# Edge lookups in adj: a bit table read by TensorE in place of 80 indirect DMAs, with host-made transposes

## The chip, the cores and the metric

One core of one Trainium2 chip runs the kernel. The metric is the device time of one execution in microseconds (us). It has five engines with their own instruction streams: PE (TensorE, matmul), DVE (VectorE), ACT (ScalarE), POOL (GpSimd) and SP (SyncE, here only a DMA queue). They wait for each other by semaphores. DMA transfers are issued from SP, ACT and POOL.

## The reference

`x` is 1354 x 512, `adj` a 0/1 matrix of 1354 x 1354 with about four other ones in a row and ones on the diagonal. The list of 10,000 edges (pairs of rows) is random; only an edge that is also in `adj` changes a softmax score, and there are fewer than 64 of those.

```python
q = (x[sub] @ Wq.T + bq).reshape(-1, 8, 64)
k = (x[obj] @ Wk.T + bk).reshape(-1, 8, 64)
att = ((q * k).sum(-1) / 8).T
scores = zeros((8, n, n)).at[:, sub, obj].set(att)
scores = where(adj == 0, -inf, scores); scores[:, i, i] = 1e-07
x1 = layernorm(x + (softmax(scores, 2).sum(0) / 8) @ x)
out = layernorm(x1 + adj @ (x1 @ W1) + b1)
```

## The kernel before, in words

Rows of `x` and `adj` stand in T = 11 tiles of 128 rows (the last has 74). Numbers that need more than fp16 are split in a high and a low half, so most products are two matmuls.

**First stage, sums.** Without edges every softmax row is uniform, so the first layer is a sum over neighbours. SP loads `adj` tile by tile into `stage` (a ring of 3), ACT casts it (L628), PE transposes it in 11 pieces (L1113), ACT copies that into `adjT` (L619). PE makes the sums of tile i with 22 matmuls of 512 columns (L1134); the first two tiles' sums are interleaved and wait for the tiles of `x` as DVE splits them (L809). DVE adds the row's own share (L884), takes its moments (L829, L830), ACT the root (L633) and the normalised row (L663), DVE splits it (`x1s`, L895 and L897).

**Second stage, mix.** 12 units of 11 steps, each step two matmuls (L1191), make `adj @ x1`: 8 units of 512 columns, then 4 of 330. `mix_rows(a, b)` in PE's program are steps a to b - 1 of these 132. ACT and DVE take each unit out of PSUM (L716, L864), four banks in turn.

**Third stage, output.** For each tile 12 matmuls with `W1` (L1273) and 2 with the rank-64 correction (L1280), then DVE adds (L1078), takes moments, ACT roots and scales (L764), and SP stores.

**Edges.** In parallel POOL looks up all 10,000 edges in `adj`: 80 indirect DMAs of 125 elements (L560), in six chunks. DVE waits for a chunk and makes flags (`flag_chunk`, L840), PE numbers the flagged edges (L481, L482) and compacts them (L489), between the work above. Each engine takes its instructions in order, so a wait for flags on DVE also holds the normalisation behind it. After the last chunk come the steps on the 64 found edges: gather rows of `x`, project (L1230), dots (L1242), softmax (L1246, exp), shares (L1250), corrected rows (`dx1`, L1056), the correction's product (L1261). They stand between steps of the mix at places written by hand. Where there are more than 64 such edges a general path runs (`overflow`); it is not taken here, but its branch is.

Of the kernel before, what the change touches and what calls it, by code (L numbers as in the profile page):

```python
# [4 lines left out]

N = 1354
# [12 lines left out]
CHUNKS = [0, 16, 32, 48, 64, 73, EC]  # L32
NC = len(CHUNKS) - 1
CHUNK = max(b - a for a, b in zip(CHUNKS, CHUNKS[1:]))

NUMBERED_AT = {4: 0, 6: 1, 8: 2, T: 3, T + 1: 4, T + 2: 5}
FLAGGED_AT = {3: 0, 5: 1, 8: 2, T - 1: 3}
# [6 lines left out]
CASTS = 2  # L44
SUMS = 4
COEFS = 4
# [10 lines left out]
def resnorm_graph(nc, x, adj, pairs, wq, bq, wk, bk, w1, b1, out):  # L57
    f32, f16, i32 = mybir.dt.float32, mybir.dt.float16, mybir.dt.int32
    ALU, ACT, AX = mybir.AluOpType, mybir.ActivationFunctionType, mybir.AxisListType
    width = [P] * (T - 1) + [LAST]  # L60

    with ExitStack() as ctx:
# [5 lines left out]

        sums_dram = nc.dram_tensor("sums_dram", [NP, GW], f32, kind="Internal").ap()
# [10 lines left out]
        stage = sb("stage", [P, RING, N])  # L80
        room16 = sb("room16", [P, CASTS * NP], f16)
        adj16 = room16[:, 0:CASTS * N].rearrange("p (c n) -> p c n", c=CASTS)
        sums = sb("sums", [P, SUMS, H])
        counts = sb("counts", [P, T, 2])
        wraw = sb("wraw", [P, 3, KF, H])
# [6 lines left out]

        co = sb("co", [P, COEFS, 8])

        st = sb("st", [P, 2, 12])
        last_st = sb("last_st", [P, 12])
        onehot = sb("onehot", [P, P * CHUNK], f16)
        stackL = sb("stackL", [P, NP], f16)
        junk16 = stackL[:, 0:P]
# [8 lines left out]
        slot_no = sb("slot_no", [P, P, CHUNK], f16)  # L108
# [8 lines left out]
        ok2 = y[:, 0, 0:2 * EC].rearrange("p (c two) -> p c two", two=2)  # L117
        ed_ok = sb("ed_ok", [P, EC])
# [3 lines left out]
        ed_adj = sb("ed_adj", [P, EC])  # L122
        ed3 = sb("ed3", [P, EC, 3], f16)
        flag = sb("flag", [P, EC], f16)
        seen = sb("seen", [P, EC])
        pos = sb("pos", [P, 3, CHUNK])
        pos16 = sb("pos16", [P, CHUNK], f16)
        pos_all = seen[0:EP]
# [7 lines left out]
        raw = wraw[:, :, :, :].rearrange("p a b c -> p (a b c)")  # L136
        at = 2 * KF * H

        def take(n):
            nonlocal at  # L140
            at += n
            return raw[:, at - n:at]
        xsub, xobj, spread, same, keq, vsame, small = map(take, (H, H, H, P, SLOTS, P, 80))
        head_of = take(2)
        assert at <= 3 * KF * H
        at = 0
        EXTRA = SLOTS + 3
# [4 lines left out]
        assert at <= 2 * KF * H  # L152
# [41 lines left out]
        idx_ready, flags_ready, numbered, onehot_ready, compacted = map(sem, ("idx_ready", "flags_ready", "numbered", "onehot_ready", "compacted"))  # L194
        wqk_transposed, wqkT_ready, count_ready = map(sem, ("wqk_transposed", "wqkT_ready", "count_ready"))
# [7 lines left out]
        biased, out_done, z_ready, z_moments, z_root = map(sem, ("biased", "out_done", "z_ready", "z_moments", "z_root"))  # L203
# [14 lines left out]

# [10 lines left out]
        ROW_STEPS = 7 + HEADS * 11 + 3 + 3  # L229
# [31 lines left out]
        def general_pe(pe):  # L261
            mm = nc.tensor.matmul
            with pe.Fori(0, T) as t:
# [47 lines left out]
            pe.wait_ge(turn, FINISHED)  # L311

# [33 lines left out]
        def general_dve(dve):  # L346
# [38 lines left out]

# [113 lines left out]
        def _(sp):  # L499
# [29 lines left out]
            with overflow(sp):  # L529
                general_sp(sp)  # L530
# [782 lines left out]
```

## Time and profile before

| what | value |
|---|---|
| median of 3 runs | 238.35 us (237.59 to 239.12) |
| span of the profiled execution | 238.4 us, 3058 instructions |
| PE busy | 186.1 us (78%) |
| DVE busy | 131.5 us (55%) |
| ACT busy | 87.4 us (37%) |
| POOL busy | 130.4 us (55%) |
| DMA | 24.59 MB, mean 103 GB/s |
| granted TensorE clock in 40 slices | `9999999998556999965785979999979999999995` |

The span is that of one execution taken by the profiler; it agrees with the median. The last line is the clock that PE was granted in each fortieth of the span, in tenths of full speed (5 is the lower of its two levels, 1.2 GHz, 9 the full 2.4 GHz). Two matmuls overlap in part, so a group's busy time is a little under its count times its mean.

### The profile page before, as it was taken

To read this page: it belongs to the slowest core of one execution; us is meant where nothing else is said; L and a number is where in the kernel's file an instruction comes from. 1 tells how busy PE (TensorE), PEld (TensorE's weight loads), DVE (VectorE), ACT (ScalarE), POOL (GpSimd) and SP (SyncE) were. 2 spreads that over 40 slices of the span, in tenths; PEclk is the share of its full clock that TensorE was granted. 3 is DMA by queue.
4 is the path that set the end of the run, shared out by engine and by line. 5 is a ranking of instruction groups with operands and counts; after the bars stand their busy time and mean duration, and the time that the engine had idled before them with its cause. 6 is when DMAs were issued, how large, how long until landed. Compare 5 with 4: busy or idle time off the path is not lost.

```text
span 238.4 us, 3058 instructions
## 1 busy us (share of the span) xinstructions
PE 186.1 (78%) x1075; PEld 100.0 (42%) x1075; DVE 131.5 (55%) x374; ACT 87.4 (37%) x153; POOL 130.4 (55%) x114
## 2 busy tenths in 40 slices
PE   4776999991089989504959799979799969999950
PEld 4533455550064554301433346934336544444440
DVE  4695877850385658004617085079897213666670
ACT  3656998960192864000511101401412211333340
POOL 3878878877778777877778654999000000000000
PEclk9999999998556999965785979999979999999995
DMA  6999996766230157820300004000000000222220
GB/s 194 399 300 320 297 331 179 190 170 104 36 90 2 46 182 243 274 62 1 47 1 4 1 21 142 3 1 0 1 0 3 0 4 5 88 91 88 89 88 25
DMA packets 14924, 24.59 MB, mean 103 GB/s; under 512 B 6012, under 2 KB 6137, under 8 KB 14903
## 3 DMA queue, kind: packets, MB, share of 16 engines
q1 hardware_dynamic: 9046, 20.34, 26.1%
q0 software_dynamic: 2848, 1.10, 5.1%
q10 hardware_dynamic: 3008, 2.90, 3.6%
q8 instruction: 10, 0.16, 0.3%
q14 instruction: 12, 0.09, 0.1%
HBM read 14.61 MB, written 9.63 MB: 102 GB/s over the span
## 4 chain that ended last, share of the span: by engine, by line
POOL 43%; PE 31%; issue 12%; DVE 8%; DMA 2%; ACT 1%; DVEq 0%; POOLq 0%
POOL ed_adj L560 43%; PE acc L1191 12%; PE acc L1273 9%; PE tr L1230 3%; PE tr L1273 2%; PE acc L1280 1%; DMA ed_adj<-in_adj,ed_idx 1%; DMA ed_i<-in_L_gnn_rel_pair_index 1%; PE tr L1261 1%; DVE wraw L989 1%; DVE st L829 1%; DVE wraw L988 1%; DVE slot L1008 1%; DVE wraw L996 0%; PE tr L1246 0%
## 5 line engine op out<-in xcount | busy, mean ns | idle before, releaser
L560 POOL DMA_INDIRECT ed_adj<-in_adj,ed_idx x80 | 104.0, 1301 | 27.4 <-issue 23.8
L1191 PE MATMUL acc<-adjT,x1s 128*128 128x512 f16 (+3 forms) x264 | 61.3, 393 | 0.0
L1134 PE MATMUL acc<-xs,adjT 128*128 128x512 f16 (+1 forms) x176 | 42.7, 399 | 2.1 <-ACT adjT L619 1.3
L1191 PEld LDWEIGHTS acc<-adjT,x1s 128*128 128x128 f16 (+1 forms) x264 | 27.0, 106 | 29.5 <-issue 11.8
L633 ACT ACTIVATE st<-st,eps 128x1 f32<-128x1 f32 x24 | 7.1, 297 | 63.1 <-DVE st L830 62.0
L1134 PEld LDWEIGHTS acc<-xs,adjT 128*128 128x128 f16 (+1 forms) x176 | 17.4, 102 | 23.7 <-issue 3.9
L1273 PE MATMUL acc<-whl,xs 128*128 128x512 f16 (+1 forms) x108 | 23.5, 368 | 2.1 <-issue 2.1
L840 DVE SCALAR_TENSOR_TENSOR flag<-ed_adj,ed_ok 125x16 f16<-125x16 f32 (+2 forms) x6 | 1.0, 173 | 41.8 <-DMA ed_adj<-in_adj,ed_idx 41.8
L1113 PE MATMUL tr<-ident,room 128*128 128x128 f16 (+1 forms) x121 | 9.2, 229 | 15.5 <-ACT room L628 14.9
L1273 PEld LDWEIGHTS acc<-whl,xs 128*128 128x128 f16 x108 | 10.5, 98 | 13.9 <-issue 2.5
L628 ACT ACTIVATE room<-stage 128x1354 f16<-128x1354 f32 x11 | 14.7, 1333 | 4.5 <-DMA stage<-in_adj 4.5
L1113 PEld LDWEIGHTS tr<-ident,room 128*128 128x128 f16 (+1 forms) x121 | 7.9, 104 | 19.4 <-ACT room L628 17.6
L619 ACT COPY adjT<-tr 128x1024 f16<-128x1024 f16 (+1 forms) x22 | 15.4, 754 | 1.8 <-PE tr L1113 1.8
L1134 PE MATMUL tr<-xs,adjT 128*128 128x512 f16 (+1 forms) x66 | 14.7, 379 | 0.0
L481 PE MATMUL acc<-flag,below 125*128 125x16 f16 (+2 forms) x6 | 1.1, 182 | 17.3 <-DVE flag L840 17.3
L608 POOL TENSOR_TENSOR x_sb<-x_sb,bias 128x512 f32 x11 | 14.4, 1346 | 0.3 <-POOL stackL L602 0.3
L716 ACT ACTIVATE xs<-acc 128x512 f16<-128x512 f32 (+1 forms) x12 | 6.3, 540 | 20.6 <-PE acc L1191 20.5
L829 DVE BATCH_NORM_STATS2 st<-y 128x6 f32<-128x512 f32 x17 | 11.8, 695 | 0.6
L864 DVE SCALAR_TENSOR_TENSOR xs<-acc,xs 128x512 f16<-128x512 f32 (+1 forms) x12 | 7.3, 620 | 5.9 <-ACT xs L716 5.9
L663 ACT ACTIVATE x_sb<-y,st 128x512 f32<-128x512 f32 x11 | 9.0, 821 | 1.1 <-DVE st L835 1.0
L1134 PEld LDWEIGHTS tr<-xs,adjT 128*128 128x128 f16 (+1 forms) x66 | 6.3, 98 | 7.1
L834 DVE RECIPROCAL st<-st 128x1 f32<-128x1 f32 x24 | 3.9, 161 | 9.1 <-ACT st L633 9.1
(195 smaller groups left out, 248.3 us busy)
## 6 DMA issues: line engine op xcount, KB each, us to landing
stage<-in_adj SPq DMA_DIRECT2D x10, 677.0 KB, 7.4
adjT_dram<-adjT SPq DMA_DIRECT2D x11, 352.0 KB, 3.0
sums_dram<-sums ACTq DMA_DIRECT2D x11, 256.0 KB, 3.6
x_sb<-in_x SPq DMA_DIRECT2D x3, 768.0 KB, 9.0
out<-y SPq DMA_DIRECT2D x6, 256.0 KB, 2.0
ed_adj<-in_adj,ed_idx POOLq DMA_INDIRECT x80, 3.4
wraw<-in_L_gnn_Wq SPq DMA_DIRECT2D x1, 1024.0 KB, 17.8
wraw<-in_L_gnn_Wk SPq DMA_DIRECT2D x1, 1024.0 KB, 10.4
```

What stands on the lines that cost most here:

```text
L560: nc.gpsimd.indirect_dma_start(out=ed_adj[0:EP, c:c + 1], out_offset=None, in_=adj_flat, in_offset=bass.IndirectOffsetOnAxis(ap=ed_idx[0:E ...
L608: nc.gpsimd.tensor_tensor(tile, tile, bias[:, :], ALU.add).then_inc(biased, 1)
L619: nc.scalar.copy(adjT[:, 8 * b:8 * b + n, t * P:(t + 1) * P], tr16[b][:, 0:n * P].rearrange("p (k i) -> p k i", k=n)).then_inc(adjT_ready, 1)
L628: nc.scalar.activation(adj16[:, t % CASTS, :], stage[:, t % RING, :], ACT.Copy, accum_out=counts[:, t, 0:1]).then_inc(adj_cast, 1)
L663: nc.scalar.activation(x_sb[:, i, :], y[:, i % 2, :], ACT.Identity, bias=st[:, i % 2, 9:10], scale=st[:, i % 2, 8:9]).then_inc(x1_ready, 1)
L829: step(V.bn_stats(s[:, 0:6], v))
L864: V.scalar_tensor_tensor(mix[:, 1, u % KF, i:j], mix_bank(u)[:, 0:j - i], 1.0 / XS, mix[:, 0, u % KF, i:j], ALU.mult, ALU.subtract).then_i ...
L1113: last = nc.tensor.transpose(tr16[b][0:width[k], (k % 8) * P:(k % 8 + 1) * P], adj16[:, t % CASTS, k * P:k * P + width[k]], ident16[:])
L1134: last = mm(sum_bank(i)[:, :], adjT[0:width[k], k, i * P:(i + 1) * P], xs[0:width[k], half, k, :], start=(k == 0 and half == 0), stop=(k = ...
L1191: ins = mm(mix_bank(u)[:, 0:j - i], x1s[0:width[k], half, k, f * P:(f + 1) * P], adjT[0:width[k], k, i:j], start=(k == 0 and half == 0), s ...
L1230: last = mm(bank[:, o * SLOTS:(o + 1) * SLOTS], wT[:, n, k, o * P:(o + 1) * P], rows_T[:, k * SLOTS:(k + 1) * SLOTS], start=(k == 0), stop ...
L1273: mm(bank, mix[:, a, k, t * P:(t + 1) * P], whl[:, b, k, columns], start=(k == 0 and n == 0), stop=False)
```

## The change

The 80 lookups go. In their place:

- The host hands over `adj` transposed in tiles (`adj_T`, padded to 1408), its diagonal, and `Wq`, `Wk` transposed. ACT casts each tile straight into `adjT` (1408 columns), and no PE transposes or ACT copies remain for `adj`, `Wq` and `Wk`.
- PE multiplies each `adj` tile with an identity scaled by powers of two (`words`, 11 matmuls of 129 columns): every element of the 128 x 128 result holds 11 bits of `adj`, one for each column tile. DVE folds the 11 results with OR (`fold`) into one table of 128 x 128 words.
- The edges' row numbers mod 128 are written to DRAM and read back onto all partitions (`hot`, 20,000 B on each), the column numbers too (`cols`, 10,000 B on each). DVE turns `hot` into one-hot columns (`hot_part`, 4 pieces). PE multiplies them with the table (`look`, 21 matmuls of 480 columns), DVE masks each by the column (`pick`, 21), PE sums each column (80 matmuls of one column each, with 125 columns of weights taken at a stride of 80 elements).
- The words hold bits of other rows too, so DVE keeps the 8 highest candidates of each partition and POOL looks up these in 8 indirect DMAs.
- The first norm is taken of x + r*S and not of the scaled row, so ACT no longer copies the sums or scales `x` (L645, L671); it now makes the high half of `x1s` as well.
- `Wq`, `Wk` and `W1` are loaded last. POOL adds the bias to `x_sb` before the lookups. In the output six products with `W1` (`base`) now stand ahead of the overflow branch, and the corrections (`finish`) behind it.

```diff
-            for c in range(EC):
-                nc.gpsimd.indirect_dma_start(out=ed_adj[0:EP, c:c + 1], ..., in_=adj_flat, ...)
+            pool.wait_ge(bias_loaded, 16 * BIASES)
+            pool.wait_ge(x1_lo, T)
+            ... (11 adds of bias)
+            pool.wait_ge(top_ready, 1)
+            for c in range(TOP):
+                nc.gpsimd.indirect_dma_start(out=found[0:EP, c:c + 1], ..., in_=adj_flat, ...)
@@ SP
+            load_adj(2)
+            sp.dma_start(aii_all, adj_diag).then_inc(diag_loaded, 16)
+            sp.wait_ge(edges_split, 1)
+            sp.dma_start(row_dram..., row16[0:EP]).then_inc(row_stored, 16)
+            sp.dma_start(col_dram..., col8[0:EP]).then_inc(col_stored, 16)
+            load_adj(3)
+            load_adj(4)
+            load_adj(5)
+            sp.wait_ge(row_stored, 16)
+            sp.dma_start(hot, row_dram.partition_broadcast(P)).then_inc(row_spread, 16)
+            load_adj(6)
+            load_adj(7)
+            sp.wait_ge(col_stored, 16)
+            sp.dma_start(cols[:, :], col_dram.partition_broadcast(P)).then_inc(col_spread, 16)
@@ ACT
+            cast_adj(0); high_x(0); cast_adj(1); high_x(1); high_x(2)
+            cast_adj(2); high_x(3); cast_adj(3)
+            for i in range(T):
+                act.wait_ge(moments_ready, i + 1)
+                act.wait_ge(coefs_ready, i + 1)
+                root(st[:, i % 2], eps_row[:, i:i + 1]).then_inc(root_ready, 1)
+                act.dma_start(sums_dram[...], y4(i)).then_inc(y_stored[i % YS], 16)
+                if i + 4 < T:
+                    cast_adj(i + 4)
+                ... (normalise, high half of x1s)
@@ DVE
+            for t in range(3):
+                split_x(t)
+            dve.wait_ge(diag_loaded, 16)
+            ... (4 small instructions on the diagonal)
+            fold(0)
+            coefs(0)
+            for t in range(3, 6):
+                split_x(t)
+            fold(1)
+            coefs(1)
+            for t in range(6, T):
+                split_x(t)
+            fold(2)
+            for i in range(T):
+                add_sums(i)
+                if i + LEAD + 1 < T:
+                    fold(i + LEAD + 1)
+                if i + 2 < T:
+                    coefs(i + 2)
+                scale_shift_of(i)
+                if i >= 1:
+                    low_x1(i - 1)
+                if 3 <= i < 3 + HOT_PARTS:
+                    hot_part(i - 3)
+                for n in LOOKS_AFTER.get(i, ()):
+                    pick(n)
+            low_x1(T - 1)
+            for n in range(picks, 15):
+                pick(n)
+            mix_low(0)
+            mix_low(1)
+            for n in range(15, LOOKS):
+                pick(n)
@@ PE
+            def look(n):
+                ...
+                if n >= 2:
+                    pe.wait_ge(picked, n - 1)
+                mm(tr[n % 2][...], table[:], hot[:, part], start=True, stop=True).then_inc(looked, 1)
+            keep_warm(40)
+            words(0); sum_neighbours(0, range(0, 3)); words(1); ...
+            words(3)
+            for i in range(2, T):
+                if i + LEAD < T:
+                    words(i + LEAD)
+                sum_neighbours(i, range(T))
+                for n in LOOKS_AFTER.get(i, ()):
+                    look(n)
+            for first, last in MIX_BEFORE_LOOKS:      # ((0, 9), (11, 20), (9, 11), (20, 33))
+                for n in range(first, last, 2):
+                    mix_rows(n, min(n + 2, last))
+                    if looks < LOOKS:
+                        look(looks)
+            mix_rows(MIX_BEFORE_LOOKS[-1][1], 36)
+            pe.wait_ge(picked, LOOKS)
+            for c in range(EC):
+                last = mm(acc[3][0:EP, WORD + c:WORD + c + 1], picked_edge[:, :, c], ones16[:, 0:1], ...)
+            mix_rows(36, 66)
+            pe.wait_ge(flags_ready, 1)
```

What DVE runs at the start of the program, before the change (`x_sb` are rows of x, `xs` their halves, `co` the coefficients of a tile; L798 is the last instruction on edges):

```order
L798 TENSOR_TENSOR ed<-ed,ed_in 125x80x2
L805 TENSOR_SCALAR xs<-x_sb 128x1536
L809 SCALAR_TENSOR_TENSOR xs<-x_sb,xs 128x512 x3
L805 TENSOR_SCALAR xs<-x_sb 128x1536
L809 SCALAR_TENSOR_TENSOR xs<-x_sb,xs 128x512 x3
L818 SCALAR_TENSOR_TENSOR stackL,counts<-room,ident 128x128
```

The same place of the changed kernel (L742 is the last on edges, L809 to L812 those on the diagonal, L754 and L755 a fold, L767 to L770 the coefficients):

```order
L742 SCALAR_TENSOR_TENSOR ed_key<-ed_key,ed_ok 125x80
L804 TENSOR_TENSOR bit_eye<-ident,co 128x11x128
L747 SCALAR_TENSOR_TENSOR xs<-x_sb,xs 128x512 x3
L809 COPY counts<-co 128x11
L810 TENSOR_SCALAR co<-co 128x11
L811 TENSOR_SCALAR co<-co 128x11
L812 SCALAR_TENSOR_TENSOR co<-co 128x11
L754 COPY counts<-tr 128x1
L755 SCALAR_TENSOR_TENSOR folded<-ident,co,tr 128x128
L767 SCALAR_TENSOR_TENSOR co<-counts,co 128x1
L770 SCALAR_TENSOR_TENSOR co<-co 128x1
L747 SCALAR_TENSOR_TENSOR xs<-x_sb,xs 128x512 x3
```

The second and third group of splits now stand behind the instructions on the diagonal, and those behind its load.

What PE runs around the start of the mix, before the change (`room` is the cast adj, `wraw` the weights, `ed` and `onehot` the edges):

```order
L1134 MATMUL acc<-xs,adjT 128x512 x22
L1166 MATMUL acc<-ident,wraw 128x128 x4
L1191 MATMUL acc<-adjT,x1s 128x512 x4
L489 MATMUL acc<-ed,onehot 128x3 x16
L481 MATMUL acc<-flag,below 128x16
L482 MATMUL acc<-flag,ones 128x16
L1191 MATMUL acc<-adjT,x1s 128x512 x34
```

And in the changed kernel (L1099 are sums, L1113 a look, with `hot` in the place of `wraw`, L1153 the mix):

```order
L1099 MATMUL acc<-xs,adjT 128x512 x22
L1113 MATMUL tr<-wraw,table 128x480 x2
L1153 MATMUL acc<-adjT,x1s 128x512 x4
L1113 MATMUL tr<-wraw,table 128x480
L1153 MATMUL acc<-adjT,x1s 128x512 x4
L1113 MATMUL tr<-wraw,table 128x480
```

The numbering and compaction in six rounds has left this place, and a look stands behind every second step of the mix until the 21st.

## Rows read from the trace of the kernel before

**Rows 1.** The page's chain that ended last, by engine.

```profile
POOL 43%; PE 31%; issue 12%; DVE 8%; DMA 2%; ACT 1%; DVEq 0%; POOLq 0%
```

**Rows 2.** The page's groups: busy us, mean ns | idle before, releaser.

```profile
L840 DVE SCALAR_TENSOR_TENSOR flag<-ed_adj,ed_ok 125x16 f16<-125x16 f32 (+2 forms) x6 | 1.0, 173 | 41.8 <-DMA ed_adj<-in_adj,ed_idx 41.8
...
L608 POOL TENSOR_TENSOR x_sb<-x_sb,bias 128x512 f32 x11 | 14.4, 1346 | 0.3 <-POOL stackL L602 0.3
```

**Rows 3.** PE's timeline in the sums: start, us, instructions, [idle before].

```profile
26.11 4.91 PE L1134 MATMUL tr<-xs,adjT 128*128 128x512 f16 x22
30.87 0.78 PE L1113 MATMUL tr<-ident,room 128*128 128x128 f16 x11
...
66.40 1.36 PE L1113 MATMUL tr<-ident,room 128*128 128x128 f16 x11 [11.78 <-ACT room L628]
```

**Rows 4.** Windows: PE, PEld, DVE, ACT, POOL busy, PEclk, DMA share, GB/s.

```profile
58.00:60.00 2.00, 0.00 (x0) 0.00 (x0) 0.00 (x0) 0.00 (x0) 1.65 (x2) 0.57 0.25 50
```

**Rows 5.** The same, of ten microseconds in which DMA was full.

```profile
10.00:20.00 10.00, 8.68 (x47) 3.79 (x45) 6.93 (x17) 5.01 (x9) 8.17 (x7) 1.00 1.05 318
```

**Rows 6.** The tile stage: its loads from SP and their time to landing.

```profile
L514 SPq DMA_DIRECT2D stage<-in_adj x9: 258/328/2781, 4.9 to 47.8; - x9
...
DMA to landing us min/median/max: 4.1/7.4/16.2
```

**Rows 7.** DVE's timeline in the first stage.

```profile
9.06 1.90 DVE L809 SCALAR_TENSOR_TENSOR xs<-x_sb,xs 128x512 f16<-128x512 f32 x3
...
26.85 0.75 DVE L884 SCALAR_TENSOR_TENSOR y<-acc,co,xd 128x512 f32<-128x512 f32 x1
...
28.36 0.18 DVE L830 BATCH_NORM_AGGREGATE st<-st 128x2 f32<-128x6 f32 x1
```

**Rows 8.** PE's timeline around chunks of edges.

```profile
110.76 10.23 PE L1191 MATMUL acc<-adjT,x1s 128*128 128x512 f16 x34
120.83 1.10 PE L489 MATMUL acc<-ed,onehot 125*128 125x3 f16 x16
...
136.43 0.18 PE L481 MATMUL acc<-flag,below 125*128 125x7 f16 x1 [1.68 <-DVE flag L840]
136.49 3.31 PE L1191 MATMUL acc<-adjT,x1s 128*128 128x512 f16 x8
```

**Rows 9.** The chain in order of time: the last lookups.

```profile
131.89 1.22 POOL ed_adj L560
133.41 2.76 DMA ed_adj<-in_adj,ed_idx
```

**Rows 10.** Weight loads of the compaction: ns min/median/max.

```profile
L489 PEld LDWEIGHTS acc<-ed,onehot x80: 140/162/179, 68.2 to 139.9; 125*128 125x128 f16 x80
```

**Rows 11.** PE's timeline behind the last chunk.

```profile
147.32 7.26 PE L1230 MATMUL tr<-wraw,wT 128*128 128x64 f32 x64
...
161.71 9.68 PE L1191 MATMUL acc<-adjT,x1s 128*128 128x512 f16 x44
173.29 1.12 PE L1250 MATMUL tr<-wraw 64*128 64x512 f32 x2 [1.89 <-DVE wraw L1037]
...
187.52 6.91 PE L1191 MATMUL acc<-adjT,x1s 128*128 128x330 f16 x48
196.54 2.77 PE L1273 MATMUL acc<-whl,xs 128*128 128x512 f16 x12 [2.12 <-issue]
```

**Rows 12.** DVE's timeline in the softmax of the found edges.

```profile
162.91 0.69 DVE L998 TENSOR_TENSOR wraw<-tr,wraw 128x512 f32<-128x512 f32 x1
...
165.78 1.22 DVE L1008 TENSOR_TENSOR slot<-wraw 128x1 f32<-128x1 f32 x1
...
172.96 0.28 DVE L1037 TENSOR_SCALAR wraw<-wraw 64x128 f32<-64x128 f32 x1
```

**Rows 13.** DVE's timeline in the output: its last two tiles.

```profile
226.97 0.69 DVE L1078 SCALAR_TENSOR_TENSOR y<-acc,x_sb 128x512 f32<-128x512 f32 x1 [0.61 <-PE acc L1280]
...
229.34 0.42 DVE L1091 SCALAR_TENSOR_TENSOR xd<-acc,x_sb 128x256 f32<-128x256 f32 x1
```

More of the change, by code:

```diff
@@ L43 @@
 RING = 3
[L44 to L46 removed]
+YS = 4
+LEAD = 2
 GW = H + 2
@@ L121, in resnorm_graph @@
         ed_idx = sb("ed_idx", [P, EC], i32)
[L122 to L128, printed above, removed]
+        ed_key = sb("ed_key", [P, EC])
+        ed_bit = sb("ed_bit", [P, EC], i32)
+        ed_word = sb("ed_word", [P, EC], i32)
+        ed_cand = sb("ed_cand", [P, EC])
+        row16 = sb("row16", [P, EC], f16)
+        col8 = sb("col8", [P, EC], u8)
+        hot = wraw[:, :].bitcast(f16)[:, 0:E]
+        cols = sb("cols", [P, E], u8)
+        top_key = sb("top_key", [P, TOP])
+        top_i = sb("top_i", [P, 4, TOP], i32)
+        found = sb("found", [P, TOP])
+        top3 = sb("top3", [P, TOP, 3], f16)
+        flag = sb("flag", [P, TOP], f16)
+        many = sb("many", [P, 1])
+        many16 = sb("many16", [P, 1], f16)
+        seen = sb("seen", [P, TOP])
+        total = sb("total", [P, 1])
+        pos = sb("pos", [P, 3, TOP])
+        pos16 = sb("pos16", [P, TOP], f16)
+        pos_all = ed_cand[0:EP]
         slot = sb("slot", [P, 16])
@@ L1065, in _ @@
                                    ALU.mult, ALU.subtract).then_inc(right_lo, 1)
-            for u in range(8, UNITS):
-                mix_low(u)
             with overflow(dve):
@@ L1122, in keep_warm, with words @@
                     mm(tr[2][:, 0:P], ones16[:], ones16[:], start=True, stop=True)
-            keep_warm(28)
-            transpose_adj(0)
-            keep_warm(24)
+            def words(t):
+                pe.wait_ge(adj_cast, t + 1)
+                if t >= 2:
+                    pe.wait_ge(words_folded, t - 1)
+                for k in range(T):
+                    last = mm(tr[t % 2][:, 0:P + 1], adjT[:, k, t * P:(t + 1) * P], bit_eye[:, k, :], start=(k == 0), stop=(k == T - 1))
+                last.then_inc(words_done, 1)
             def sum_neighbours(i, ks):
@@ new lines, in _ @@
+            for t in range(2, OUTS):
+                pe.wait_ge(mix_lo, (9, 10, 11, 12)[t - 2])
+                base(out_bank(t)[:, :], t, everything).then_inc(based, 1)
+                if t == 3:
+                    pe.wait_ge(dT_lo, 1)
+                    for k in range(KF):
+                        for n, (a, b) in enumerate(((0, 0), (0, 1), (1, 0))):
+                            last = mm(tr[2][0:64, :], dT[:, a, k * SLOTS:(k + 1) * SLOTS], whl[:, b, k, :],
+                                      start=(k == 0 and n == 0), stop=(k == KF - 1 and n == 2))
+                    last.then_inc(dS_done, 1)
@@ new lines, with lay_out @@
+_INS = ['x', 'adj', 'L0_gnn_rel_pair_index', 'L0_gnn_bq', 'L0_gnn_bk', 'L1_gnn_weight', 'L1_gnn_bias', 'adj_T', 'L0_gnn_Wq_T', 'L0_gnn_Wk_T', 'adj_diag']
+def lay_out(inputs):
+    laid = dict(inputs)
+    adj = np.asarray(inputs["adj"])
+    padded = np.zeros((NP, NP), adj.dtype)
+    padded[:N, :N] = adj
+    laid["adj_T"] = padded.reshape(T, P, T, P).transpose(0, 3, 2, 1).reshape(T, P, NP)
+    laid["adj_diag"] = np.diagonal(padded).reshape(T, P).T
+    for name in ("L0_gnn_Wq", "L0_gnn_Wk"):
+        laid[name + "_T"] = np.asarray(inputs[name]).T
+    return laid
```

678 lines of the change are left out of this document (300 added, 378 removed).

## Prediction

> **What bounds the kernel now.** I read the chain that ended last first. POOL holds 43% of it and PE 31% [rows 1]: the 80 lookups. Then the groups with the idle time before them: DVE stood 41.8 us waiting for looked-up chunks [rows 2]. Then PE's timeline, since what PE loses is what counts once POOL has left the chain: it stood 11.8 us in front of a transpose at 66.4 [rows 3], because DVE, held by a chunk, freed no tile, and again before 110.8. The last lookup lands at 133.41 + 2.76 = 136.2, PE numbers it at 136.4 [rows 8, 9], and from there the 60-odd found edges, the rest of the mix and the output run with little idle to 238.4. The lookups also cost clock: 34 mix matmuls behind the second wait took 10.2 us, where 44 take 9.7 at the full clock [rows 8, 11]. So a kernel without them is bound by PE, with DVE just behind it, and the question is how much of its 102 us after 136.4 moves forward, and what waits come in.
>
> **Prices.** Full clock: a mix step of two 512-column matmuls 0.433 us, one of 330 columns 0.288 (44 in 9.68, 48 in 6.91 [rows 11]); sums of a tile 4.76 (26.11 to 30.87), `words` 0.63, as the 11 transposes of 128 columns have it [rows 3]; a look of 480 columns 0.2. DVE: a split 0.64 [rows 7], adding sums with moments 1.7 (26.85 to 28.54 [rows 7]); a pick reads PSUM for 480 columns, so like a split, 0.65; a fold 0.7 and coefficients 0.8, estimates from small rows of 0.15 to 0.28 each.
>
> **Stage 1, to the sums of tile 2.** DVE now does 19 instructions on edges and 1,408 columns of `bit_eye` (about 1.5), then splits three tiles: done at about 12.3. Then it waits for the diagonal, which SP issues right behind adj tile 2. That tile's load was issued at 4.9 and took 16.2, the longest: landed at 21.1 [rows 6], in a stretch in which DMA was full at 318 GB/s [rows 5]. The new kernel asks for nearly the same bytes before it, without the lookups. I take 20.5. Behind this wait stand the splits of tiles 3 to 10, and PE's first two sums need all of them: 0.8 for the diagonal, fold and coefficients 1.3, three splits to 24.5, fold and coefficients, five splits to 29.2. PE, done with the first three tiles of both sums, is idle from about 14.7 to 23.2 and comes back at the low clock, as it did after its 11.8 us (granted 0.57 in the idle time, then 11 transposes in 1.36 for 0.78 [rows 3, 4]). It ends tile 0 at 32.6 and tile 1 at 33.5. The cast of tile 4 stands behind the root of tile 0 on ACT: sums added 34.7, root 35.1, cast 36.5, `words` 37.1. **Sums of tile 2 start at 37.1**, against 26.1 [rows 3]: 11 us lost. The Trainium skill (DMA: Bandwidth & Descriptors, Queues, rings and completion order) says that an engine consumes one issuer's descriptors in ring order; by that the small diagonal can't overtake, and the landing in [rows 6] is the measure to use. It also says completion is not FIFO, so by it alone an early diagonal isn't excluded.
>
> **Stage 2, nine sums, six `words`, six looks:** 42.8 + 3.8 + 1.2 = 47.8, to 84.9. DVE has 4.2 us of work in a 5.4 us cycle, 5 to 7 with a `hot_part` of 0.7 to 2.6, and has two tiles of slack. `adj` tile 6 stands behind the 2.56 MB of `hot`: at 318 GB/s [rows 5] 8 us after 22.5, and it is needed at 43.
>
> **Stage 3, 36 mix steps, 15 looks, the column sums.** 15.6 + 3.0. Look 6 comes after two steps, but needs pick 4, which DVE reaches only after adding tile 10's sums (1.7), its root and scale (0.8), a split and the pick: 3.9 us against 1.3 on PE, so a wait of 2.6. Look 17 comes right after unit 1 is complete and needs pick 15, which stands behind `mix_low(1)`: 0.6 ACT, 0.7 and 0.65 DVE, 2.2. The 80 column sums: the compaction's 16 took 0.061 each from start to start [rows 8], its weight loads 0.162 each if not overlapped [rows 10]. Bounds 4.9 and 13.0; the reads are alike but for a longer stride, so I take 6.4. The Trainium skill (TensorE: Matmul & The Clock Gate, Weight-path perf modes) grants the fast weight load to 128 weights only; these are 125, and by its P/1.2 the 80 would be an estimated 8.3, a total 2 us later. Sum 29.8, to **114.7**.
>
> **Stage 4, the eight lookups.** DVE: thirteen small instructions, 2.9. POOL: 0.3, seven times 1.51, and 2.76 to the last landing [rows 9]; flag and number 0.3 [rows 8]: 14.0. Together 16.9. The 30 mix steps that cover it take 13.0, so PE waits 4 us: to **131.6**. What POOL did before is over by then: 11 bias adds of 1.35 [rows 2] end near 105.
>
> **Stage 5, to the first correction.** 22 steps of 0.433 and 44 of 0.288: 22.2. Small products 12.4: the projection 7.1 [rows 11], shares and score spread 1.1 each [rows 11], and by their shapes the first spread 0.5, dots and row sum 0.9, transposes 1.2, numbering and compaction 0.6. Six products with W1, 2.77 busy and so some 2.6 apart [rows 11], and the correction's at 2.7: 18.3. The branch 2.1, now behind them [rows 11]. Waits 3.0: small ones around the gathers and dots 1.1, and the softmax. There DVE took 10.3 us from the spread scores to the shares (162.91 to 173.24 [rows 12]); 0.9 goes with two instructions, and 1.8 because instructions like the 1.22 us one on 128 x 1 [rows 12] ran beside POOL's bias adds, which are done by now. 7.6 against 5.5 on PE: 1.9. After the 4 us wait the clock falls; before, 34 matmuls lost 2.9 (10.23 for the 7.4 of 17 steps [rows 8]): 2.8. Sum 60.8, to **192.4**.
>
> **Stage 6, the output.** Six tiles' products are done, so PE isn't the bound but DVE: one tile in 2.37 (226.97 to 229.34 [rows 13]). The first correction 0.45, ten tiles 23.7, and from the start of the last tile to the end 9.06 (238.4 - 229.34): 33.2, where before it was 41.9 from 196.54. PE needs 18 of it. **192.4 + 33.2 = 225.6, say 226**, against 238.4; the median stands where the profiled span does.
>
> **The rivals.** (a) As summed, 226 (0.42), own range 221 to 231. (b) The diagonal doesn't hold DVE: it lands before 14. Then the first sums end near 25, the cast of tile 4 gives 29.0 in place of 37.1: 218 (0.17). For it: 44 bytes a partition; against it, its place in the queue. (c) The three short waits (2.6, 2.2, 1.9) each drop the clock. Before, waits of 1.7 and 1.9 did so and 2.1 didn't; 8 matmuls behind one took 3.31 for 1.73 [rows 8]. Three of 1.8: 231 (0.15). (d) The column sums take 13.0: 232 (0.12). (e) Both, 237: the time is as before within 1% (0.07). (f) Slower: the spreads onto all partitions run slowly. All 128 partitions read one 20,000 B row, and the trace has a stretch where DMA moved 50 GB/s with a quarter of its engines busy [rows 4]. `adj` tiles 6 to 10 stand behind them on SP. At 50 GB/s `hot` takes 51 us, ends at 74 in place of being needed at 41, and `cols` costs 26 more: about 280. It costs nothing down to 140 GB/s; it decides (over 238) at about 80. (0.07.) Against it: nothing ties that stretch to such a read, and rows of 5,416 B ran at 318 GB/s [rows 5].
>
> **How the numbers follow.** About 1% can be told from no change. (a) to (d) are faster by over 1%, less a little for their upper edges: 0.82. Same 0.09, from (e) and those edges. Slower 0.09, from (f) and what I haven't seen in so many new waits. The range 217 to 236 reaches from (b) through (d).
>
> **What would show it.** DVE idle from 12 to 20 in front of the diagonal, with the sums of tile 2 at 37 (29 says (b)). PE's mix starting near 86; waits of 2 to 3 us in front of looks 6 and 17 and no others; column sums of 6 us; POOL's eight lookups 12 us long with PE waiting 4 us; DVE 2.4 us a tile in the output, without idle. Wrong would be: PE waiting for casts in the sums (f), column sums over 10 us (d), or the fold and pick instructions costing twice their price, which would make DVE the bound of stages 2 and 3.

## The result and the profile after

The changed kernel takes 248.98 us (median, 245.79 to 249.39), beside 237.97 for the kernel before on the same chip: a ratio of 1.0427, 95% interval 1.0362 to 1.0492. It is 4.3% slower where 226 us, 5% faster, was predicted. The profiled execution spans 244.9 us, before 238.4; its own time is 246.79, since the time of an execution is 1.7 to 1.9 us above its span in these runs. Stages are compared by the span.

The page of the changed kernel shows in two parts where the time went: its forty slices (tenths of busy time, and the clock granted to PE), and its costliest groups (busy us, mean ns, idle before).

```profile
PE   5392959999999959699999997999969999999500
DVE  3916684688887697660000422720689231287870
PEclk9866897999999999996555699999995999999965
```

```profile
L1153 PE MATMUL acc<-adjT,x1s 128*128 128x512 f16 (+3 forms) x264 | 59.6, 377 | 0.0
L1170 PEld LDWEIGHTS acc<-ones,wraw 128*125 128x125 f16 x80 | 25.1, 425 | 0.1
L1170 PE MATMUL acc<-ones,wraw 128*125 128x1 f16 x80 | 25.0, 450 | 0.0
L587 POOL DMA_INDIRECT found<-in_adj,top_i x8 | 9.8, 1224 | 34.8 <-DVE top_i L890 32.7
L878 DVE CAST ed_word<-acc 125x80 int32<-125x80 f32 x1 | 0.2, 241 | 25.5 <-PE acc L1170 25.5
```

The 80 lookups are gone, and with them the 41.8 us that DVE waited for them [rows 2]; eight are left, 9.8 us long. In their place stand the 80 column sums of L1170. They keep PE for 25.0 us, with one moving column each (the column that is streamed past the 125 loaded ones), and their weight loads alone are busy for all of it. DVE has nothing to do in that time (slices 19 to 22), and PE's clock falls to half. PE's timeline gives the marks (start, length, what, idle time before it and its releaser; rows chosen):

```profile
22.93 7.29 PE L1099 MATMUL acc<-xs,adjT 128*128 128x512 f16 x24 [5.10 <-DVE xs L747]
35.76 0.82 PE L1090 MATMUL tr<-bit_eye,adjT 128*128 128x129 f16 x11 [2.52 <-ACT adjT L621]
36.42 6.60 PE L1099 MATMUL tr<-xs,adjT 128*128 128x512 f16 x22
...
85.97 1.02 PE L1153 MATMUL acc<-adjT,x1s 128*128 128x512 f16 x4
89.61 0.36 PE L1113 MATMUL tr<-wraw,table 128*128 128x480 f16 x1 [2.61 <-DVE wraw L793]
...
109.58 25.02 PE L1170 MATMUL acc<-ones,wraw 128*125 128x1 f16 x80
134.46 15.61 PE L1153 MATMUL acc<-adjT,x1s 128*128 128x512 f16 x60
151.57 0.18 PE L1174 MATMUL acc<-flag,below 125*128 125x8 f16 x1 [1.51 <-DVE flag L898]
...
183.72 1.94 PE L1224 MATMUL tr<-wraw 64*128 64x512 f32 x2 [2.12 <-DVE wraw L1011]
192.30 2.75 PE L1230 MATMUL acc<-whl,xs 128*128 128x512 f16 x12
...
211.88 0.59 PE L1241 MATMUL acc<-stackR,stackL 128*128 128x512 f16 x2 [0.57 <-issue]
```

Stage by stage, each from one of these starts to the next:

| stage | predicted us | measured us |
|---|---|---|
| 1, to the sums of tile 2 | 37.1 | 36.4 |
| 2, nine sums, six looks | 47.8 | 49.6 |
| 3 without the column sums | 23.4 | 23.6 |
| 3, the column sums | 6.4 | 24.9 |
| 4, eight lookups, to the numbering | 16.9 | 17.1 |
| 5, to the first correction | 60.8 | 60.3 |
| 6, the output | 33.2 | 33.0 |
| sum | 225.6 | 244.9 |

In the span the miss is 19.3 us, and 18.5 of it is one row of the table (the median misses by 23: it lies above the profiled span). What follows asks why 80 weight loads cost four times their price, and whether the rest of the sum holds once they don't.

### The profile page after: what moved, and what is told of

It reads as the page before. It is cut to its first block, busy times and chain, and to the rows that moved or that the text cites. A ratio compares the mean times of both kernels' runs of the same rounds, so it can differ in the third digit from the quotient of the medians.

```text
span 244.9 us, 2922 instructions
## 1 busy us (share of the span) xinstructions
PE 205.6 (84%) x1051; PEld 118.9 (49%) x1051; DVE 130.3 (53%) x378; ACT 68.4 (28%) x107; POOL 31.8 (13%) x53
## 4 chain that ended last, share of the span: by engine, by line
PE 61%; DVE 17%; DMA 6%; issue 4%; POOL 4%; SPq 3%; ACT 3%; DVEq 0%; ACTq 0%
PE acc L1099 15%; PE acc L1153 12%; PE acc L1170 10%; PE tr L1099 7%; PE acc L1230 5%; DMA co<-in_adj_diag 5%; DVE st L774 4%; POOL found L587 4%; PE tr L1202 3%; PE tr L1090 2%; DVE y L1051 2%; PE tr L1113 2%; ACT st L626 2%; SPq L497 2%; DMA found<-in_adj,top_i 1%
## 5 line engine op out<-in xcount | busy, mean ns | idle before, releaser
L1153 PE MATMUL acc<-adjT,x1s 128*128 128x512 f16 (+3 forms) x264 | 59.6, 377 | 0.0
L1099 PE MATMUL acc<-xs,adjT 128*128 128x512 f16 (+1 forms) x176 | 43.1, 403 | 5.1 <-DVE xs L747 5.1
L1153 PEld LDWEIGHTS acc<-adjT,x1s 128*128 128x128 f16 (+1 forms) x264 | 27.0, 105 | 27.8 <-issue 5.0
L1099 PEld LDWEIGHTS acc<-xs,adjT 128*128 128x128 f16 (+1 forms) x176 | 17.8, 103 | 26.7 <-DVE xs L747 6.3
L1170 PEld LDWEIGHTS acc<-ones,wraw 128*125 128x125 f16 x80 | 25.1, 425 | 0.1
L1170 PE MATMUL acc<-ones,wraw 128*125 128x1 f16 x80 | 25.0, 450 | 0.0
L1230 PE MATMUL acc<-whl,xs 128*128 128x512 f16 (+1 forms) x108 | 23.2, 367 | 0.0
L621 ACT CAST adjT<-stage 128x1408 f16<-128x1408 f32 x11 | 15.0, 1363 | 8.4 <-DMA stage<-in_adj_T 7.7
L1099 PE MATMUL tr<-xs,adjT 128*128 128x512 f16 (+1 forms) x66 | 16.4, 410 | 0.0
L793 DVE SCALAR_TENSOR_TENSOR wraw<-cols,row_no,tr 128x480 f16<-128x480 uint8 (+1 forms) x21 | 14.3, 708 | 3.0 <-PE tr L1113 3.0
L1090 PE MATMUL tr<-bit_eye,adjT 128*128 128x129 f16 x121 | 10.1, 238 | 6.8 <-DVE bit_eye L804 4.2
L587 POOL DMA_INDIRECT found<-in_adj,top_i x8 | 9.8, 1224 | 34.8 <-DVE top_i L890 32.7
L1090 PEld LDWEIGHTS tr<-bit_eye,adjT 128*128 128x128 f16 x121 | 8.8, 107 | 9.6 <-DVE bit_eye L804 4.4
L626 ACT ACTIVATE st<-st,co 128x1 f32<-128x1 f32 x11 | 3.2, 294 | 33.5 <-DVE st L775 33.4
L799 DVE SCALAR_TENSOR_TENSOR xs<-acc,xs 128x512 f16<-128x512 f32 (+1 forms) x12 | 7.3, 626 | 8.8 <-ACT xs L661 8.7
L1113 PE MATMUL tr<-wraw,table 128*128 128x480 f16 (+1 forms) x21 | 7.2, 364 | 4.7 <-DVE wraw L793 4.7
L1099 PEld LDWEIGHTS tr<-xs,adjT 128*128 128x128 f16 (+1 forms) x66 | 6.8, 104 | 8.3 <-issue 2.2
L626 ACT ACTIVATE st<-st,eps 128x1 f32<-128x1 f32 x13 | 3.8, 295 | 22.0 <-DVE st L775 20.9
## 6 DMA issues: line engine op xcount, KB each, us to landing
wraw<-row_dram SPq DMA_DIRECT2D x1, 2500.0 KB, 11.7
```

Source lines behind the costliest of these rows:

```text
L587: nc.gpsimd.indirect_dma_start(out=found[0:EP, c:c + 1], out_offset=None, in_=adj_flat, in_offset=bass.IndirectOffsetOnAxis(ap=top_i[0:EP, ...
L621: nc.scalar.copy(adjT[:, :, t * P:(t + 1) * P], stage[:, t % RING, :].rearrange("p (k i) -> p k i", k=T)).then_inc(adj_cast, 1)
L626: return nc.scalar.activation(s[:, 10:11], s[:, 7:8], ACT.Sqrt, bias=floor)
L793: V.scalar_tensor_tensor(hot[:, part], cols[:, part], row_no[:, 0:1], bank[:, 0:part.stop - part.start], ALU.is_equal, ALU.mult).then_inc( ...
L1090: last = mm(tr[t % 2][:, 0:P + 1], adjT[:, k, t * P:(t + 1) * P], bit_eye[:, k, :], start=(k == 0), stop=(k == T - 1))
L1099: last = mm(sum_bank(i)[:, :], adjT[0:width[k], k, i * P:(i + 1) * P], xs[0:width[k], half, k, :], start=(k == 0 and half == 0), stop=(k = ...
```

## The experiments

The kernels below change the changed kernel, unless it says otherwise. "Before" in each is the unchanged kernel on the same chip.

**128 weight columns in place of 125.** Theory A says that the count of columns makes the load slow, theory B the stride of 160 bytes between them.

```diff
+            step(V.memset(wraw[:, :].bitcast(f16)[:, E:P * EC], 0.0))
...
-            picked_edge = hot.rearrange("q (p c) -> q p c", p=EP)
+            picked_edge = wraw[:, :].bitcast(f16)[:, 0:P * EC].rearrange("q (p c) -> q p c", p=P)
...
-                last = mm(acc[3][0:EP, WORD + c:WORD + c + 1], picked_edge[:, :, c], ones16[:, 0:1], start=True, stop=True)
+                last = mm(acc[3][:, WORD + c:WORD + c + 1], picked_edge[:, :, c], ones16[:, 0:1], start=True, stop=True)
```

> The 80 column sums load 128 weight columns in place of 125, at the same stride of 80 values; the three extra ones come from 240 zeroed values behind the edges. Theory A (the count of weight columns makes the load slow; 128 strided columns took 0.06 us from start to start in the compaction): the 80 take 5 to 7 us, the granted clock stays up, and the time falls by 18 to 21 us, to 228 to 231. Theory B (the stride of 160 bytes between the weights makes it slow): still 24 to 26 us, time unchanged at 248 to 250.

229.88 us, ratio to before 0.965 (0.9599 to 0.9701). PE's timeline:

```profile
112.80 6.50 PE L1171 MATMUL acc<-ones,wraw 128*128 128x1 f16 x80
119.16 15.88 PE L1154 MATMUL acc<-adjT,x1s 128*128 128x512 f16 x60
```

The 80 take 6.4 us from start to start (112.80 to 119.16), the 6.4 that the prediction gave them, and the kernel is now faster than before. Three more columns of work make the step four times shorter: the count matters. Whether the stride does too, this run alone can't say. One part of the expectation missed: the clock did not stay up, the window from 119 to 124 has it at 0.50.

**125 columns beside each other.** The other side of the same question.

```diff
-                last = mm(acc[3][0:EP, WORD + c:WORD + c + 1], picked_edge[:, :, c], ones16[:, 0:1], start=True, stop=True)
+                last = mm(acc[3][0:EP, WORD + c:WORD + c + 1], hot[:, EP * c:EP * (c + 1)], ones16[:, 0:1], start=True, stop=True)
```

> 125 weight columns again, but beside each other in memory in place of 160 bytes apart (each sum then belongs to other edges than it is filed under; the amount of work is the same). Theory A (count of columns): the 80 stay at 24 to 26 us and the time near 248. Theory B (stride): 5 to 7 us, the time 228 to 231. If both this and the run with 128 columns are fast, either alone is enough; if both are slow, neither explains it and the load of a fresh 125-row operand with one moving column is slow as such.

```profile
108.92 4.74 PE L1170 MATMUL acc<-ones,wraw 128*125 128x1 f16 x80
113.53 14.81 PE L1153 MATMUL acc<-adjT,x1s 128*128 128x512 f16 x60
130.64 0.18 PE L1174 MATMUL acc<-flag,below 125*128 125x8 f16 x1 [2.31 <-DVE flag L898]
```

225.35 us (one execution, and with sums that belong to other edges): 4.6 for the 80, 0.058 each. So neither theory alone: 125 columns are fast side by side, a 160-byte stride is fast with 128, and only both together are slow.

**One column sum in place of 80**, to see the stages behind it without it.

```diff
-            step(V.tensor_copy(word, acc[3][0:EP, WORD:WORD + EC]))
+            step(V.tensor_copy(word, acc[3][0:EP, WORD:WORD + 1].broadcast_to([EP, EC])))
...
-            for c in range(EC):
+            for c in range(1):
                 last = mm(acc[3][0:EP, WORD + c:WORD + c + 1], picked_edge[:, :, c], ones16[:, 0:1], start=True, stop=True)
```

> Only 1 of the 80 column sums is issued, its column is read for all 80; the kernel leaves out 79/80 of that step. Theory A (the step costs its 25 us and the clock it takes with it): the time falls by 25 us for the step and 1 to 3 for the 60 mix matmuls behind it, less up to 2 that PE then waits for the lookups: 221 to 225. Rival (DVE or the lookups are behind it and bound the stage anyway): a fall of less than 20 us.

```profile
109.18 0.26 PE L1170 MATMUL acc<-ones,wraw 128*125 128x1 f16 x1
109.30 13.12 PE L1153 MATMUL acc<-adjT,x1s 128*128 128x512 f16 x60
126.39 0.19 PE L1174 MATMUL acc<-flag,below 125*128 125x8 f16 x1 [3.98 <-DVE flag L898]
```

Its time as a whole says nothing. The execution takes 2,343 us, for the kernel takes its general branch: the costliest lines of its page, L301 to L433, are of that branch. Presumably, with one word for all 80 edges of a partition, more edges pass for found than there are slots. The expectation about the end isn't tested. Up to the numbering it can be read: 60 mix matmuls take 13.1 us where they took 15.6 behind the slow sums, so those cost another 2.5 in clock; and PE waits 3.98 for the lookups, where the prediction had 4. In the changed kernel that wait was 1.51, because the mix matmuls, slow at the low clock, covered the rest. The 2.5 of clock and the 2.5 less of waiting cancel, and that is why stage 4 came out as predicted.

**Which loads are slow.** The kernel with 128 columns, with 13 groups of 16 single-column products added, each group behind 24 products of 512 columns (`warm`).

```diff
+            for count, stride in ((124, 80), (126, 80), (127, 80), (120, 80), (96, 80), (64, 80), (125, 1), (125, 2), (125, 16), (125, 40), (124, 2), (128, 80), (125, 80)):
+                warm()
+                for c in range(16):
+                    last = mm(acc[3][0:count, at + c:at + c + 1],
+                              wraw[:, :].bitcast(f16)[:, c:c + count * stride:stride] if stride > 1 else hot[:, 128 * c:128 * c + count],
+                              ones16[:, 0:1], start=True, stop=True)
+                at += 16
...
```

> As the run with 128 weight columns, with 13 groups of 16 single-column products more behind the column sums, each behind 24 warming products of 512 columns, all on the same data: 124, 126, 127, 120, 96 and 64 weight columns 160 bytes apart, then 125 columns 2, 4, 32 and 80 bytes apart, 124 columns 4 bytes apart, 128 and 125 columns 160 bytes apart. It does more work than the kernel and its whole time says nothing; the start-to-start times of each group do. Known: 125 at 160 bytes 0.31 us each, 128 at 160 bytes 0.080, 125 side by side 0.058. Theory A1 (only 128 columns are fast once they are strided): 124, 126, 127, 120, 96, 64 all take 0.15 to 0.31, 125 slow at every stride above one value. Theory A2 (a strided load is fast when its count divides by four): 124, 120, 96, 64 near 0.06 to 0.08, 126 and 127 slow. Theory B2 (long strides are slow unless there are 128 columns): 125 at 4 and 32 bytes fast, at 80 and 160 slow.

PE's timeline; a group's cost is the start of the warming products behind it less its own start (shown for the first). In `128*124` the second number is the count of weight columns. The three rows of 125 columns from 194.96 on have them 2, 4 and 32 bytes apart, the last row 160:

```profile
126.87 4.96 PE L1181 MATMUL acc<-ones,wraw 128*124 128x1 f16 x16
131.69 6.86 PE L1176 MATMUL tr<-x1s,ident 128*128 128x512 f16 x24
...
185.43 2.72 PE L1181 MATMUL acc<-ones,wraw 128*64 128x1 f16 x16
...
194.96 1.04 PE L1181 MATMUL acc<-ones,wraw 128*125 128x1 f16 x16
...
201.04 1.07 PE L1181 MATMUL acc<-ones,wraw 128*125 128x1 f16 x16
...
207.15 3.66 PE L1181 MATMUL acc<-ones,wraw 128*125 128x1 f16 x16
...
233.32 1.37 PE L1181 MATMUL acc<-ones,wraw 128*128 128x1 f16 x16
...
239.73 4.96 PE L1181 MATMUL acc<-ones,wraw 128*125 128x1 f16 x16
```

| columns | bytes apart | us each |
|---|---|---|
| 64, 96, 120 | 160 | 0.166, 0.228, 0.288 |
| 124, 125, 126, 127 | 160 | 0.301, 0.301, 0.301, 0.308 |
| 128 | 160 | 0.077 |
| 125 | 80, 32 | 0.217, 0.220 |
| 125 | 4, 2 | 0.058, 0.057 |
| 124 | 4 | 0.058 |

At 160 bytes every count but 128 is slow, by about 2.4 to 2.6 ns a column, so even half the columns cost twice what 128 do. In the count that is A1; A2 (counts that divide by four) is out. In the stride both theories missed once: A1 had 125 columns slow at every stride above one value, and at 4 bytes they are fast; B2 had them fast at 32 bytes, and there they are slow. Between 4 and 32 bytes nothing was measured for fewer than 128 columns.

**The diagonal's load second on SP's queue**, right behind the edge list, with the column sums left slow.

```diff
             sp.dma_start(ed_i[0:EP], pairs.rearrange("(p c) two -> p c two", p=EP)).then_inc(edges_loaded, 16)
+            sp.dma_start(aii_all, adj_diag).then_inc(diag_loaded, 16)
...
             load_adj(2)
-            sp.dma_start(aii_all, adj_diag).then_inc(diag_loaded, 16)
```

> The load of the adjacency diagonal is issued second on SP's queue, right behind the edge list, in place of behind adj tile 2. Theory A (DVE is held only by its place in the queue): it lands before 8 us, the 7.4 us wait of DVE goes, the sums of tile 2 start at 28 to 30 in place of 36.4, all of it reaches the end: 7 to 8 us less, 241 to 242. Rival (small and bought back later: the casts or hot's spread become what PE waits for): less than 4 us of it reaches the end, with PE waits in the nine sums.

242.68 us, ratio to before 1.0196 (1.0122 to 1.0269), where the changed kernel's is 1.0427: 2.3%, or 5.5 us, between the 7 to 8 of the theory and the 4 of its rival. DVE no longer waits for the diagonal. What it and PE wait for now, first on DVE and ACT, then on PE:

```profile
24.10 1.29 DVE L747 SCALAR_TENSOR_TENSOR xs<-x_sb,xs 128x512 f16<-128x512 f32 x2 [4.27 <-ACT xs L631]
22.18 1.36 ACT L621 CAST adjT<-stage 128x1408 f16<-128x1408 f32 x1 [5.01 <-DMA stage<-in_adj_T]
23.45 1.15 ACT L631 ACTIVATE xs<-x_sb 128x512 f16<-128x512 f32 x2
```

```profile
30.17 1.38 PE L1090 MATMUL tr<-bit_eye,adjT 128*128 128x129 f16 x11 [1.22 <-ACT adjT L621]
31.34 7.32 PE L1099 MATMUL tr<-xs,adjT 128*128 128x512 f16 x22
```

The sums of tile 2 start at 31.3, not at 28 to 30: ACT scales x tiles 9 and 10 only behind the cast of `adj` tile 2, which lands at 22. So 5.1 us came forward, and all but 0.7 of it stayed: the mix starts at 81.61, 4.4 us earlier. No PE wait for a cast came into the nine sums.

**Both, and looser cover.** The first of three kernels has 128 columns and the early diagonal; the second 128 columns and looser cover; the third all. "Looser cover" is: look 6 comes after ten mix steps in place of two, `mix_low(0)` and `mix_low(1)` come behind all picks, and the numbering comes after mix row 71 in place of 66, with the small products behind it moved likewise.

```diff
-            for n in range(picks, 15):
+            for n in range(picks, LOOKS):
                 pick(n)
             V.memset(mix[:, :, :, N:NP], 0.0)
             mix_low(0)
             mix_low(1)
-            for n in range(15, LOOKS):
-                pick(n)
...
-                    if looks < LOOKS:
+                    pairs_done += 1
+                    if pairs_done > 4 and looks < LOOKS:
...
-            mix_rows(36, 66)
+            mix_rows(38, 71)
```

> Both earlier edits at once: 128 weight columns, and the diagonal's load second on SP's queue. Theory (the two costs are independent, the first 19.1 us and the second 6.3 us as measured apart): 229.9 less 4 to 6.5 is 223.5 to 226. Rival (the two overlap, since a front that is early only waits longer for hot, cols or the lookups): 227 to 230.

> 128 weight columns, and looser cover: look 6 comes after ten mix steps in place of two, both low halves of the mix come behind all picks on DVE, the numbering five mix steps later. Theory (the waits of 2.6, 2.1 and 1.2 us and the clock drops behind them cost what they last, and the mix steps that are done in them are missing nowhere): 229.9 less 4 to 7, 223 to 226. Rival (the waits only move, to the first correction or the softmax): above 227.5.

> 128 weight columns, the diagonal's load second on the queue, and the looser cover together. Theory (three independent costs): 217 to 221, faster than the kernel before by 7 to 9%. Rival (the lookups or DVE become the bound once PE has no waits): 222 to 226.

Measured: 224.06 (0.9352, interval 0.9237 to 0.9467), 222.23 (0.9337, 0.9271 to 0.9402) and 216.89 (0.9105, 0.9037 to 0.9173). The run with 128 columns alone was on another chip, so compare spans of profiled executions: from its 228.1 the early diagonal takes 5.6, the cover 7.0, both 12.3. The ratios to before (from 0.965) give 7.1, 7.4 and 13.0 us. Within their intervals the parts add. The cover ended just below its forecast of 223 to 226. Not all of it was a gain: a part of the waits moved, as its rival had it. PE's wait in the softmax grew from 2.11 to 2.67, and behind it stands a new one of 1.23 for `mix_low` (L799). In the third kernel PE's timeline has no wait from the sums of tile 2 to the dots of the found edges; there it reads:

```profile
99.58 6.50 PE L1171 MATMUL acc<-ones,wraw 128*128 128x1 f16 x80
105.94 17.27 PE L1152 MATMUL acc<-adjT,x1s 128*128 128x512 f16 x66
123.06 0.18 PE L1175 MATMUL acc<-flag,below 125*128 125x8 f16 x1
```

The 66 mix matmuls take 17.1 us, where they take 14.3 at the full clock (0.433 for two), though PE waited for nothing ahead of them. The low clock comes with the 80 single-column products here too (granted 0.74 from 104 to 106, in their last part), as the window behind them has it (busy times of PE, PEld, DVE, ACT, POOL, then the granted clock):

```profile
106.00:110.00 4.00, 4.00 (x11) 1.41 (x11) 3.14 (x17) 0.00 (x0) 1.31 (x1) 0.50 0.02 4
```

**The output loop, and ACT's order in the front.** Both on top of the third kernel. The first asks whether the output is bound by DVE's chain, as predicted; the second whether ACT's order is what held the front in the run with the early diagonal.

```diff
+            add_out(0)
             for t in range(T - 1):
...
                 moments(st[:, t % 2], y4(t)).then_inc(z_moments, 1)
+                if t + 1 < T - 1:
+                    add_out(t + 1)
                 dve.wait_ge(z_root, t + 1)
```

> The kernel with 128 weight columns, early diagonal and looser cover, and in the output loop DVE adds the next tile's product before it waits for ACT's root of this one. Theory (the output is bound by DVE, 2.37 us a tile of which 0.36 is its wait for the root): about 0.36 less for each of nine tiles, 3 to 4 us, 213 to 214. Rival (PE's products or the stores bound the output behind tile 5): 0 to 1 us less.

```diff
-            cast_adj(2)
             high_x(3)
+            cast_adj(2)
             cast_adj(3)
+            cast_adj(4)
```

> As the one before, and ACT scales x tiles 9 and 10 ahead of the cast of adj tile 2, and casts adj tile 4 ahead of the first root. Theory (with the diagonal early, what holds the front is ACT's order: tiles 9 and 10 behind the landing of adj tile 2 at 21.9, and the cast of tile 4 behind the first root, PE waits of 0.44 and 2.85): 2 to 4 us less, 209.5 to 212. Rival (adj tiles 3 and 4 land late too, so the bytes bound the front): under 1 us less.

Measured: 211.32 (0.8779, 0.8712 to 0.8846) and 207.69 (0.8637, 0.8581 to 0.8692). DVE's timeline in the output of the first:

```profile
196.80 0.69 DVE L1048 SCALAR_TENSOR_TENSOR y<-acc,x_sb 128x512 f32<-128x512 f32 x1
197.41 0.15 DVE L779 RECIPROCAL st<-st 128x1 f32<-128x1 f32 x1
197.59 0.21 DVE L780 TENSOR_SCALAR st<-st 128x1 f32<-128x1 f32 x1
197.72 0.69 DVE L774 BATCH_NORM_STATS2 st<-y 128x6 f32<-128x512 f32 x1
198.44 0.18 DVE L775 BATCH_NORM_AGGREGATE st<-st 128x2 f32<-128x6 f32 x1
198.55 0.69 DVE L1048 SCALAR_TENSOR_TENSOR y<-acc,x_sb 128x512 f32<-128x512 f32 x1
```

A tile takes 1.75 us (196.80 to 198.55) in place of 2.33 in the third kernel (183.41 to 192.73 in four tiles). The wait for the root, 0.36, is covered by the next tile's add. Another 0.22 goes, since instructions that don't need each other start before the one ahead has ended: the reciprocal at 197.41, where the add of 196.80 ends at 197.49. From the first correction to the end it is 27.8 us in place of 33.0, 5.2 less, where 3 to 4 were expected. PE's products, 3.02 a tile, didn't become the bound, because six tiles were ready. The second kernel gave 3.6 more: the sums of tile 2 start at 27.70, so up to there the bytes are not the bound. Further on they begin to be: a cast waits 6.83 us for the landing of an `adj` tile, up to 37.79, and PE then 1.20 for that cast, a wait that the kernels above don't have.

```profile
27.04 0.82 PE L1095 MATMUL tr<-bit_eye,adjT 128*128 128x129 f16 x11 [0.65 <-ACT adjT L621]
27.70 2.54 PE L1104 MATMUL tr<-xs,adjT 128*128 128x512 f16 x11
```

At 207.69 us it is 13.6% faster than the kernel before, on the same idea as the change.

## Why the prediction was wrong, point by point

- **The step that failed: the price of the column sums, "the reads are alike but for a longer stride, so I take 6.4".** The two bounds were one-hot loads at 0.061 and 0.162 each [rows 8, 10], and both rows have 128 weight columns, 32 bytes apart. For 125 columns 160 bytes apart no row of before had a price, and the stride was waved through. It measured 24.9 us, nearly twice the upper bound of 13.0, and over the 10 us that the prediction named as its sign of being wrong. That bound came from rows of another form and was no bound.
- **The rule of the Trainium skill** (TensorE: Matmul & The Clock Gate, Weight-path perf modes), that the fast load is given only to 128 weights, pointed the right way: at this stride 128 are fast and 125 aren't. Its price doesn't fit: P/1.2 (same page, LDWEIGHTS) makes 0.104 each, the runs show 0.301 to 0.311 at 160 bytes apart and 0.057 side by side. It knows no stride, so it gives the side-by-side run the same 0.104, and that one was the fastest. The measurements decide: the count and the stride together make the cost. I gave the rule one sentence and no rival; the only warning sign on this term was not followed to its question, how a strided load of fewer columns is priced.
- **Stage 1 right:** the diagonal landed at 20.3 (20.5), PE came back at 22.93 (23.2), the sums of tile 2 started at 36.42 (37.1). The early-diagonal run shows the cause: with the diagonal early, DVE doesn't wait for it. Rival (b)'s price of 8 us was too high by about 3: it forgot that ACT had put x tiles 9 and 10 behind `adj` tile 2.
- **Stage 2 short by 1.8:** the sums of tile 2 ran partly at the low clock. PE had its clock back by 30, stood 2.52 us before 35.76, which the prediction had in its times without a cost in clock, and was granted 0.72 from 36.4 to 38 and 0.50 from 38 to 40. The 22 matmuls at 36.42 took 6.4 from start to start, not 4.8.
- **Stage 3's waits right:** 2.61 and 2.12 for 2.6 and 2.2. The run with looser cover, which has neither, is the faster for it.
- **Rival (c), that each of three short waits drops the clock,** happened in one place of three in the changed kernel: granted 1.00 behind the waits of 2.61 and 2.12, 0.50 behind the one in the softmax. In the run with 128 columns it did behind the first two as well:

```profile
92.00:94.00 2.00, 2.00 (x6) 0.76 (x5) 0.71 (x1) 0.00 (x0) 2.00 (x3) 0.50 1.08 371
...
104.00:108.00 4.00, 3.67 (x10) 1.40 (x11) 2.23 (x4) 0.00 (x0) 0.42 (x1) 0.57 0.02 4
```

  (windows of that run: PE, PEld, DVE, ACT, POOL busy, granted clock, DMA share, GB/s). With the column sums at 6.4 it ended at 229.9, between rivals (a) and (c). The probe kernel lost clock behind both, the one with the early diagonal and 128 columns behind the first alone. The prediction's own reading was too narrow here: in the kernel before, a wait of 1.68 that ended at 136.43 dropped the clock, but one of 1.70 that ended at 160.54 didn't (granted 1.00 from 160 to 166). What decides whether such a wait costs clock stays open.
- **Stage 4:** right in length. PE's wait was 1.51, not 4; the 3.98 appears once the mix steps run at full clock. That the parts cancelled is luck.
- **Stage 5 right in sum, by luck in its parts:** the branch took 0.57 in place of 2.1. The 2.8 for a low clock behind the lookups didn't come (granted 1.00 from 150 to 156). In its place the clock fell behind the softmax wait: the product at 183.72 took 1.86 from start to start where 1.05 is the full clock's, the 30 mix matmuls behind it 6.7 for 4.3, together 3.2. That wait was 2.12; the prediction's own terms, 7.6 less 5.5, make 2.1, not the 1.9 that it took.
- **Stage 6 right,** and right in its cause: DVE's chain, at 2.31 to 2.37 a tile. Rearranging it shortened the output.
- **Rivals (d), (e) and (f):** (d) named the right term with too low a price, and so did (e), which adds (c) to it. (f), slow spreads, didn't happen: `hot` landed in 11.7 us and `cols` in 8.0, and no PE wait came of it.

## What to carry to other kernels

Price an instruction only from a row with its own shape: the count of weight columns and the stride between them, not just "a weight load". Where no such row exists, the nearest one is no upper bound, and a step that is repeated 80 times deserves the widest range of all. Filling up this strided weight operand to 128 columns cost one clearing of 0.16 us on DVE and was worth some 19 us.

A wait in a stage with other work ready can be taken away by order alone: those for the diagonal, for picks 4 and 15 and the flags, for the root in the output and for ACT's casts gave some 22 us together (229.9 to 207.7), without one instruction less. Look at the new trace each time, though: the wait for the flags, gone in the third kernel, is back with 1.24 and 1.05 us in the last two, where the mix steps ahead of it ran at the low clock for a shorter time. Ask of each which engine's order, not which engine's speed, makes it.

## What the hardware showed that I had not expected

- A weight load of 64 to 127 fp16 columns 160 bytes apart, with the one-column product behind it, takes 2.4 to 2.6 ns a column, 0.30 us for 125, while 128 such columns take 0.077; 125 side by side or 4 bytes apart take 0.058, 32 bytes apart 0.220. No run took the load apart from its product, or shows what in the load makes the difference.
- The slow loads hardly depend on the granted clock. 16 of them took 4.82 us (0.301 each) at 0.97, and the changed kernel's 80 took 24.9 (0.311 each), most of them at 0.50. Windows of the probe and of the changed kernel:

```profile
126.90:131.70 4.80, 4.80 (x18) 4.80 (x18) 0.00 (x0) 0.00 (x0) 0.00 (x0) 0.97 0.00 0
```

```profile
108.00:112.00 4.00, 4.00 (x18) 3.22 (x15) 1.15 (x1) 0.60 (x1) 0.00 (x0) 1.00 0.00 0
112.00:114.00 2.00, 2.00 (x8) 2.00 (x7) 0.00 (x0) 0.00 (x0) 0.00 (x0) 0.55 0.00 0
114.00:134.00 20.00, 20.00 (x65) 20.00 (x65) 0.00 (x0) 0.00 (x0) 0.00 (x0) 0.50 0.00 1
134.00:138.00 4.00, 4.00 (x11) 1.77 (x12) 2.99 (x17) 0.00 (x0) 0.79 (x1) 0.50 0.00 0
```

- PE is shown 100% busy from 109.6 on, and yet its clock fell at about 112 from 2.4 to 1.2 GHz, and was still there at 138, with the mix steps running again since 134.5. PE busy with weight loads and single-column products didn't hold the clock: an engine shown busy can be granted half of it. The fast loads didn't hold it either: with 125 columns side by side it was 0.66 in the five microseconds behind them. In the probe the 24 products of 512 columns took 5.2 us, granted 1.00, behind the 16 fast loads of 128 columns, but 6.7 at 0.77 behind 16 slow ones of 124.
